# Where the bf16 parts of q and k are made: one adaLN block with attention and experts

## The reference

```python
mod = (silu(c) @ wmod).reshape(8, 6, 1, 128)       # sa, ca, ga, sb, cb, gb
h = layernorm(x) * (1 + ca) + sa
q, k, v = split(h @ w_qkv)                         # 16 heads of 8
attn = softmax(q @ k.T / sqrt(128))
x = x + ga * ((attn @ v) @ w_out)
h = layernorm(x) * (1 + cb) + sb
x = x + gb * moe(h)                                # softmax router, top 2 of 8, silu(g) * u
```

## Time and profile before

| | |
|---|---|
| median of 3 runs | 685.91 us (685.17 to 688.14) |
| span of the profiled execution | 679.4 us (no other time of it is listed) |
| PE busy | 618.9 us, 91% |
| DVE busy | 550.1 us, 81% |
| ACT busy | 450.5 us, 66% |
| POOL busy | 267.2 us, 39% |

### The profile page before, as it was taken

One profiled execution on the slowest core, in us unless ns is written; L12 is line 12 of the kernel. 1 busy time (PEld: TensorE's weight loads), 2 busy tenths in 40 slices (PEclk: granted clock), 3 DMA queues, 4 the chain that ended last, 5 costly groups with the idle time before them and its releaser, 6 DMA issues.

```text
span 679.4 us, 13009 instructions
## 1 busy us (share of the span) xinstructions
PE 618.9 (91%) x3413; PEld 285.7 (42%) x3413; DVE 550.1 (81%) x1065; ACT 450.5 (66%) x859; POOL 267.2 (39%) x384
## 2 busy tenths in 40 slices
PE   5299999999999999999999999889899999999995
PEld 3112223323323322322322322225667777777773
DVE  3698889899888988988988988714788888888885
ACT  2107878778778778778778777876554555555553
POOL 4522022222222222222122122333567776776773
PEclk9658999999999999999999999979899999999999
DMA  7703505304304304303403400253334454345411
GB/s 183 197 31 82 183 3 117 106 20 106 117 19 95 126 17 95 127 17 79 143 18 72 150 18 4 76 167 109 92 114 139 137 142 141 130 137 150 136 35 31
DMA packets 48972, 65.58 MB, mean 97 GB/s; under 512 B 9432, under 2 KB 30432, under 8 KB 48928
## 3 DMA queue, kind: packets, MB, share of 16 engines
q1 hardware_dynamic: 46304, 64.32, 33.1%
q10 hardware_dynamic: 2624, 0.79, 0.5%
HBM read 47.26 MB, written 17.83 MB: 96 GB/s over the span
## 4 chain that ended last, share of the span: by engine, by line
PE 34%; DVE 20%; issue 19%; POOL 16%; ACT 5%; DMA 2%; SPq 1%; DVEq 1%; POOLq 0%; ACTq 0%
POOL hid_lo L612 13%; DVE negmax L864 13%; PE o_acc L1172 11%; PE s_row L1149 10%; PE s_col L1162 5%; ACT probs L656 3%; DVE probs L1042 1%; POOL h_lo L618 1%; PE misc L1130 1%; PE misc L1103 1%; PE misc L1100 1%; SPq L325 1%; DVE sums_inv L883 1%; DVE k_rest L878 1%; PE misc L1126 1%
## 5 line engine op out<-in xcount | busy, mean ns | idle before, releaser
L864 DVE TENSOR_REDUCE negmax<-s_row 128x1 f32<-128x512 f32 x512 | 323.0, 683 | 47.5 <-PE s_row L1149 41.9
L656 ACT ACTIVATE probs<-s_col 128x512 f32<-128x512 f32 x512 | 270.8, 599 | 76.4 <-PE s_col L1162 73.4
L1149 PE MATMUL s_row<-k_stack,q_stack 64*128 64x512 bf16 x512 | 141.7, 402 | 25.2 <-DMA k_stack<-k_scr 11.6
L612 POOL TENSOR_TENSOR hid_lo<-probs,hid_hi 128x512 fp32r<-128x512 f32 x87 | 128.5, 1493 | 61.9 <-ACT hid_hi L800 61.9
L1162 PE MATMUL s_col<-q_stack,k_stack 64*128 64x512 bf16 x512 | 132.4, 383 | 7.1 <-ACT probs L656 6.5
L1172 PE MATMUL o_acc<-probs,v_aug 128*32 128x512 f32 x1024 | 138.1, 612 | 0.0
L800 ACT ACTIVATE hid_hi<-probs 128x512 fp32r<-128x512 f32 x88 | 55.6, 632 | 85.0 <-DVE probs L1042 84.6
L1149 PEld LDWEIGHTS s_row<-k_stack,q_stack 64*128 64x128 bf16 x512 | 34.9, 93 | 180.1 <-DVE negmax L864 142.1
L1042 DVE TENSOR_TENSOR probs<-probs,q_stack 128x512 f32<-128x512 f32 x56 | 62.5, 1116 | 15.7 <-POOL hid_lo L612 13.6
L520 POOL CAST negmax_parts<-negmax 128x16 bf16<-128x16 f32 x32 | 6.3, 196 | 163.0 <-DVE negmax L864 163.0
L1032 DVE TENSOR_TENSOR probs<-probs,s_col 128x512 f32<-128x512 f32 x88 | 59.6, 677 | 2.9 <-ACT probs L820 1.6
(11 more groups left out here) (134 smaller groups left out, 713.9 us busy)
## 6 DMA issues: line engine op xcount, KB each, us to landing
q_scr<-q_parts SPq DMA_DIRECT2D x48, 128.0 KB, 2.4
k_scr<-k_parts SPq DMA_DIRECT2D x48, 128.0 KB, 2.4
q_stack<-q_scr SPq DMA_DIRECT2D x8, 768.0 KB, 6.1
k_stack<-k_scr SPq DMA_DIRECT2D x8, 768.0 KB, 7.5
q_stack<-combT_scr SPq DMA_DIRECT2D x24, 256.0 KB, 3.4
k_stack<-combT_scr SPq DMA_DIRECT2D x16, 224.0 KB, 2.9
q_stack<-combT_scr SPq DMA_DIRECT2D x16, 192.0 KB, 2.7
q_stack<-combT_scr SPq DMA_DIRECT2D x16, 160.0 KB, 2.6
```

What stands on the lines that cost most here:

```text
L612: nc.gpsimd.tensor_tensor(hid_lo[k % HIDDEN][:], weighed[(par + k) % 2], hid_hi[k % HIDDEN][:], ALU.subtract).then_inc(s["hid_split"], 1)
L656: nc.scalar.activation(probs[t % 2][:, j, :], s_col[score_bank("col", u)][:], ACT.Exp, scale=INV_SCALE).then_inc(s["exp_done"], 1)
L864: nc.vector.tensor_reduce(negmax[n % 2][:, j, qc:qc + 1], s_row[score_bank("row", u)][:], AX.X, ALU.max, negate=True).then_inc(s["row_max" ...
L1149: nc.tensor.matmul(s_row[score_bank("row", u)][:], q_stack[par][at:at + KS, head // 2, P * qc:P * (qc + 1)], k_stack[par][at:at + KS, head ...
```

## The change

The first batch is split as before. For the others, ScalarE copies q (and one slot later k) from PSUM unrounded into q_rest (k_rest), and GpSimd makes all three parts out of it: round to high, subtract high in place, round to middle, subtract for low. VectorE's subtractions and ScalarE's middle copies go. PSUM's bank is free when ScalarE's copy is done. ScalarE now waits, before that copy, for the split of the batch before; GpSimd waits for that batch's stores.

```diff
+            def split(b, n, rest, high, middle, low):
+                pool.wait_ge(s[f"{n}_rest_ready"], b + 1)
+                pool.wait_ge(s[f"{n}_stored"], 16 * STORES * b)
+                pool.sem_inc(s["waited"])
+                nc.gpsimd.tensor_copy(high, rest[:]).then_inc(s[f"{n}_high"], 1)
+                pool.wait_ge(s[f"{n}_high"], b + 1)
+                nc.gpsimd.tensor_tensor(rest[:], rest[:], high, ALU.subtract).then_inc(s[f"{n}_step"], 1)
+                pool.wait_ge(s[f"{n}_step"], b)
+                pool.sem_inc(s["waited"])
+                nc.gpsimd.tensor_copy(middle, rest[:]).then_inc(s[f"{n}_mid"], 1)
+                low_part(b, low, rest, middle, f"{n}_mid", f"{n}_split")
...
-                    low_q(b + 1)
+                    split_q(b + 1)
                 if not last:
-                    low_k(b + 1)
+                    split_k(b + 1)
...
                     if not (isinstance(b, int) and b == 0):
-                        act.wait_ge(s["q_stored"], 16 * STORES * b)
-                    nc.scalar.activation(q_parts[:, Q_HIGH, :], misc_f, ACT.Copy).then_inc(s["q_high"], 1)
+                        act.wait_ge(s["q_split"], b)
+                        nc.scalar.activation(q_rest[:], misc_f, ACT.Copy).then_inc(s["q_rest_ready"], 1)
+                    else:
+                        nc.scalar.activation(q_parts[:, Q_HIGH, :], misc_f, ACT.Copy).then_inc(s["q_high"], 1)
...
-                        if at == MIDDLE_Q and not last:
-                            middle_part(b + 1, q_parts[:, Q_MID, :], q_rest, "q_rest_ready", "q_mid")
-                        if at == MIDDLE_K and not last:
-                            middle_part(b + 1, k_parts[:, K_MID, :], k_rest, "k_rest_ready", "k_mid")
...
-            REST = {(1, 2): "q", (2, 2): "k"}
...
-                            if (t, j) in REST and not last:
-                                evacuate(None, b + 1, 1 - par, REST[t, j])
```

More of the change, by code:

```diff
@@ L273, in adaln_block @@
             ln1_bn ln1_mv ln1_step ln1_ready ln1_scaled xn_ready
-            hT_ready q_high k_high q_rest_ready k_rest_ready q_mid k_mid q_split k_split v_ready
+            hT_ready q_high k_high q_rest_ready k_rest_ready q_mid k_mid q_split k_split q_step k_step v_ready
             q_stored k_stored stacked_first stacked
@@ L561, in low_k, with split_q, split_k @@
                 low_part(b, k_parts[:, K_LOW, :], k_rest, k_parts[:, K_MID, :], "k_mid", "k_split")
+            def split(b, n, rest, high, middle, low):
[9 more added lines that the diff above has]
+                low_part(b, low, rest, middle, f"{n}_mid", f"{n}_split")
+            def split_q(b):
+                split(b, "q", q_rest, q_parts[:, Q_HIGH, :], q_parts[:, Q_MID, :], q_parts[:, Q_LOW, :])
+            def split_k(b):
+                split(b, "k", k_rest, k_parts[:, K_HIGH, :], k_parts[:, K_MID, :], k_parts[:, K_LOW, :])
             pool.wait_ge(s["half_ready"], 1)
@@ L690, in evacuate @@
                     if not (isinstance(b, int) and b == 0):
-                        act.wait_ge(s["k_stored"], 16 * STORES * b)
-                    nc.scalar.activation(k_parts[:, K_HIGH, :], k_bank(b), ACT.Copy).then_inc(s["k_high"], 1)
+                        act.wait_ge(s["k_split"], b)
+                        nc.scalar.activation(k_rest[:], k_bank(b), ACT.Copy).then_inc(s["k_rest_ready"], 1)
+                    else:
+                        nc.scalar.activation(k_parts[:, K_HIGH, :], k_bank(b), ACT.Copy).then_inc(s["k_high"], 1)
                 elif name == "v":
@@ L744, in _ @@
                     place_max(0, 0, int(name[3:]))
-            MIDDLE_Q, MIDDLE_K, ROUTER_EXP, FIRST_BLOCK = (2, 0), (3, 0), (12, 0), (14, 1)
+            ROUTER_EXP, FIRST_BLOCK = (12, 0), (14, 1)
             STORE_MAX = {(1, 0): 1, (5, 0): 2, (9, 0): 3, (13, 0): 0}
@@ L869, in evacuate @@
                 if name == "q":
-                    dve.wait_ge(s["q_high"], b + 1)
-                    if not (isinstance(b, int) and b == 0):
-                        dve.wait_ge(s["q_split"], b)
+                    dve.wait_ge(s["q_high"], 1)
                     nc.vector.tensor_tensor(q_rest[:], misc_f, q_parts[:, Q_HIGH, :], ALU.subtract).then_inc(s["q_rest_ready"], 1)
                 elif name == "k":
-                    dve.wait_ge(s["k_high"], b + 1)
-                    if not (isinstance(b, int) and b == 0):
-                        dve.wait_ge(s["k_split"], b)
+                    dve.wait_ge(s["k_high"], 1)
                     nc.vector.tensor_tensor(k_rest[:], k_bank(b), k_parts[:, K_HIGH, :], ALU.subtract).then_inc(s["k_rest_ready"], 1)
@@ L998, in body @@
                         name = TASKS.get(at)
-                        if name in tasks(first, last) and name not in REST.values():
+                        if name in tasks(first, last) and name not in ("q", "k"):
                             of = owner(b, name)
```

## The result

The changed kernel takes 691.28 us (median of 4 runs, 691.11 to 693.02), the kernel before 685.72 (4 runs). The ratio is 1.0091, with a 95% interval of 1.006 to 1.0122: slower, by 5.6 us, under one per cent, where 684.2 us had been forecast. The profiled execution of it has a span of 691.2 us and a time of 693.02, so 1.8 us lie outside the span. By that the execution whose span of 679.4 us was read for the prediction took about 681 us, one of the quick ones: in later runs of the same kernel the times went from 680.5 to 693.2 us.

What follows compares the result with a forecast made beforehand. TensorE and VectorE were taken as both near full, handing work to each other. Six bodies times 0.28 us plus 0 gave 1.7 us less: 677.7 + 6.5 = 684.2 us, range 679.5 to 690.5.

Steps and rivals of the forecast that it cites:

- What goes: Work removed per attention body: VectorE's q_rest and k_rest, 0.69 and 0.68 us, and two ScalarE copies, 0.63 us each.
- rival 2: GpSimd misses group 2's max split and TensorE waits: 693.4 us, or 687.8 with casts at 0.95 us; chance 0.15.
- q_rest worth nothing: In the attention body, TensorE has other work before the maxima q_rest holds up, so VectorE would idle there: 0 us.
- k_rest worth 0.28 us a body: TensorE's half slot behind k_rest shrinks from 0.83 to 0.55 us; six bodies give 1.7 us.
- Rival 1: k_rest's whole 0.68 us returns in seven bodies, 681.1 us; with q_rest too, 676.3 us; chance of both together 0.27.
- The cast: GpSimd's copy of 128x512 to bf16 in the split: 0.67 us taken, ends 0.30 and 1.154 us.
- The subtraction: GpSimd's subtraction in the q and k splits: 1.154 us taken, ends 1.04 and 1.49 us.
- Up to the middle part: GpSimd's time for one tensor's split until its middle part is ready: 2.83 us, of 3.98 us in all.
- GpSimd in time for the max split: GpSimd finishes group 2's max split, queued behind split_k, 0.7 us before TensorE needs it: cost 0.
- Stores and loads: SyncE's k stores and stack loads go 1.6 us later, with 3 us of slack left before TensorE's rows: cost 0.
- The first body at 0: In the first batch's body, the transpose goes 0.4 us behind its moved place, spending a gain of some 0.3 us: 0.
- The base: Median of the runs lies 6.5 us over the profiled span of 679.4 us, taken as fixed start and end.

Runs made afterwards that it cites:

- the kernel of the same length: Changed kernel with four or ten semaphore increments where q_rest and k_rest stood, giving VectorE's first body and loop their earlier instruction counts: 680.52 us, ratio 0.9928.
- the start at 256: Changed kernel with 64 semaphore increments at the very start of VectorE's program, so its loop starts at instruction 256: bodies with the jump 53.91 and 52.79 us.
- start 193: Changed kernel with one semaphore increment ahead of VectorE's attention loop, which then starts at instruction 193: span 687.2 us, bodies with the jump 52.59 and 52.33 us.
- the one with the moved start: Changed kernel with four semaphore increments ahead of VectorE's attention loop, which starts at 196 as before but stays ten instructions shorter: 682.16 us, ratio 0.994.

## Why the prediction was wrong

The failed step is in "What goes", a term put at nothing without a reason. VectorE's two removed subtractions were priced by the gap that they leave in TensorE's work, 0 and 0.28 us a body, which came out right. That instructions go out of VectorE's program with them (subtractions, waits and register work, four ahead of the loop and ten in it), and that everything behind them moves, was priced at nothing. The sum took the jump back as the same. Taking them out moved the loop's start from 196 to 192, and the two jumps to it cost 5.0 and 3.3 us. The two runs that move only the start, in either kernel, show it: four empty instructions more make the changed kernel 9 us faster, four fewer make the kernel before 10 us slower. Without the move the change is a gain (ratio 0.994), with it a loss (1.0091). None of the rivals had this mechanism; rival 2 would have given the right sign for a wrong reason.

The 11.8 us between the two profiled spans: 0.3 before the first copy of v, 0.9 in the first two intervals, 8.3 in the two jumps, -1.0 in the other three loop bodies, 3.4 in the last stretch, -0.2 behind it. Of the 0.9, 0.4 is the wait for the first load. The 3.4 is no effect of the change that these runs show. In that stretch the granted clock falls for longer or shorter, in kernels with and without spells; its windows, before, in the kernel of the same length, after, and with the start at 256:

```profile
390.55:472.01 81.46, 71.96 (x443) 23.62 (x441) 48.28 (x122) 62.76 (x120) 25.92 (x46) 0.96 0.26 72
```

```profile
390.41:469.73 79.32, 69.34 (x443) 23.47 (x442) 48.29 (x122) 62.62 (x120) 25.81 (x46) 1.00 0.27 74
```

```profile
399.17:484.03 84.86, 76.15 (x443) 23.44 (x441) 48.29 (x122) 62.99 (x121) 25.93 (x46) 0.90 0.24 69
```

```profile
394.00:482.10 88.10, 80.36 (x443) 24.69 (x441) 48.31 (x122) 63.19 (x121) 26.00 (x46) 0.85 0.24 67
```

The stretch with the same 443 matmuls takes 79.3 us at a mean clock of 1.00 and 88.1 at 0.85, and that is why the span at start 193 was 687.2 us (87.6 us in this stretch). It is likely most of the spread of a kernel's runs too: of the 29 executions of the kernel before, one of 680.5 us has a mean clock of 0.969 over the whole run and one of 690.3 us has 0.945. That this part of the run makes it was seen only in the one profile of each kernel. Why the clock falls there in one execution and not in another is open.

The other steps:
- q_rest worth nothing, k_rest worth 0.28 us a body: right, 0.00 and 0.25 measured by putting work back, although k_rest stood on the chain with 0.68 us. Rival 1 is refuted. VectorE is busy for 1.1 us less in a body that is 0.26 us shorter, as forecast. From the third copy of v to the eighth, five bodies, the kernel of the same length is 1.25 us shorter than before, the one with the moved start 1.44: the forecast 5 x 0.28.
- The cast: 0.61 us for 0.67, from two small sizes; the dearer one of 0.77 that the prediction set beside it did not come. The subtraction: right. Up to the middle part the sum counted three gaps for two, 2.83 us; 2.62 were measured (266.58 to 269.20).
- GpSimd in time for the max split: right, with 1.3 us of room instead of 0.7, because from q's copy to the end of both splits 7.9 us passed and not 8.5; its load alone costs nothing in the loop.
- Stores and loads: k's stores follow q's with no pause (269.23 and 273.15 in after) and start 1.3 us later behind the copy of v than before (1.6 forecast); no TensorE wait for a stack beyond the first: right.
- The first body at 0: right to some 0.5 us, as told above.
- The base: taking 6.5 us around the span as fixed was wrong. It is 1.8 us; the rest was the profiled execution being a quick one.

Of the kernels built, the one of the same length (680.52 us) and the one with the moved start (682.16) are faster than both given kernels, the kernel before at 685.78 beside them. The loop bodies account for 1.3 to 1.4 us of the 5.3 and 3.6; the intervals reach down to 1.8 and 1.6 us, and how much more than the bodies' share is real is open.

## What to carry to other kernels

Read work off the timeline and not off the chain alone: an instruction on the chain is worth only the gap that it leaves in the fullest engine, here 0.28 of 0.68 us. But an edit ahead of an engine's loop also moves that loop in the engine's program; here that was worth 8.3 us, with a loop of 362 or 372 instructions. Compare the body that holds the jump back with one that doesn't, look for idle time with the releaser "issue" and for more packets in the instruction queue, and if they are there, pad ahead of the loop by a few empty instructions before judging the edit.

## What the runs showed of the hardware

- The jump back of VectorE's loop of 362 or 372 instructions is followed by 4.18 to 4.65 us of standing still when the loop starts at instruction 192 or 320, by 1.95 to 2.25 us at 256 or 260, and by nothing that shows at 193 or 196 (0.33 us, a wait for TensorE, in the timelines shown). Ten or eleven more instruction packets are moved in the whole run at the first four, 4 or 5 instead of 2 or 3 around each jump.
- After such a spell, with TensorE nearly idle for 4 us, its granted clock was 0.51 in the next 4 us and 0.64 in the 4 after, so that the body's 322 matmuls took 2.2 us longer (51.84 for 49.68), on top of 2.9 us more of standing idle.
- GpSimd: cast float32 to bf16 over 128x512 0.61 us; subtraction with a bf16 operand, float32 or bf16 out, 1.16 us; two float32 operands 1.04 us (each of the pair above).
